# A planned order for the first and the last groups of a graph-attention layer, with Wq loaded by chunks and part of the weight work on GpSimd

## The reference, cut to what matters

```
h = maximum(layernorm(x), 0)
q, k, v = heads(h @ Wq + bq), heads(h @ Wk + bk), heads(h @ Wv + bv)
scores = q @ k.T / sqrt(64) + where(adj, 0, -9e15)
ctx = softmax(scores) @ v
out = x + ctx @ Wf + bf
```

## Time and profile before

| | |
|---|---|
| median of three runs | 478.66 us (477.88 to 484.44) |
| profiled execution: span from its first to its last instruction | 475.7 us |
| median less that span | 2.96 us |
| PE (TensorE matmul) busy | 460.9 us, 97% |
| DVE, ACT, POOL busy | 369.5, 364.8, 299.7 us |

### The profile page before, as it was taken

How to read it: one execution, slowest core, us unless ns; L and a number is a source line. 1 busy time by engine, 2 the same in 40 slices (tenths; PEclk the granted TensorE clock), 3 DMA queues, 4 the chain that set the end, 5 groups by cost and what they waited for, 6 DMA issues and landing times.

```text
span 475.7 us, 12878 instructions
## 1 busy us (share of the span) xinstructions
PE 460.9 (97%) x4454; PEld 275.6 (58%) x4454; DVE 369.5 (78%) x744; ACT 364.8 (77%) x813; POOL 299.7 (63%) x300
## 2 busy tenths in 40 slices
PE   4998999999999999999999999999999999999996
PEld 2854555556556564655657465565746556464763
DVE  4799997888679587786968778695786889677955
ACT  3677998789678877777888777887878968876950
POOL 3077576777676566686656678575767657634862
PEclk9799999999999999999999999999999999999999
DMA  8138599979969799795959969595978959966796
GB/s 294 66 83 162 97 167 170 161 154 194 210 108 199 167 160 230 132 221 116 221 119 198 199 122 227 112 222 92 191 176 129 263 109 162 217 107 148 137 197 169
DMA packets 219727, 78.56 MB, mean 165 GB/s; under 512 B 199584, under 2 KB 219680, under 8 KB 219680
## 3 DMA queue, kind: packets, MB, share of 16 engines
q1 hardware_dynamic: 209056, 65.43, 70.8%
q10 hardware_dynamic: 10624, 12.53, 9.9%
HBM read 16.19 MB, written 12.58 MB: 60 GB/s over the span
## 4 chain that ended last, share of the span: by engine, by line
PE 86%; DMA 4%; SPq 4%; DVE 2%; issue 1%; ACT 1%; POOL 1%; ACTq 0%; DVEq 0%
PE ps_proj L915 24%; PE ps_proj L917 24%; PE ps_proj L916 24%; PE ps_scores L997 6%; PE ps_ctx L915 2%; PE ps_ctx L916 2%; DMA pt_parts<-probs_parts 2%; PE ps_ctx L917 2%; SPq L474 2%; SPq L466 2%; DMA x_sb<-in_x 1%; DMA ht_parts<-h_pairs 1%; SPq L456 1%; DVE masked L751 0%; PE ps_ctx L1068 0%
## 5 line engine op out<-in xcount | busy, mean ns | idle before, releaser
L543 POOL TENSOR_TENSOR probs_parts<-probs,probs_parts 128x768 f16<-128x768 f32 x64 | 105.5, 1648 | 28.2 <-ACT probs_parts L645 28.1
L630 ACT ACTIVATE probs<-masked,neg_max 128x128 f32<-128x128 f32 x384 | 118.4, 389 | 2.3 <-DVE neg_max L760 2.1
L915 PE MATMUL ps_proj<-ht_parts,w_hi 128*128 128x512 f16 (+1 forms) x309 | 111.3, 364 | 3.3 <-DVE w_lo L833 2.0
L916 PE MATMUL ps_proj<-ht_parts,w_hi 128*128 128x512 f16 (+1 forms) x309 | 111.3, 364 | 0.0
L917 PE MATMUL ps_proj<-ht_parts,w_lo 128*128 128x512 f16 (+1 forms) x309 | 111.3, 364 | 0.0
L611 ACT ACTIVATE qkt_hi<-ps_proj,bias_qk 128x512 f16<-128x512 f32 x94 | 63.6, 682 | 37.9 <-PE ps_proj L917 37.2
L549 POOL TENSOR_TENSOR ctx_parts<-ctx_sb,ctx_parts 128x384 f16<-128x384 f32 x62 | 56.8, 917 | 53.3 <-ACT ctx_parts L651 53.0
L734 DVE SCALAR_TENSOR_TENSOR qkt_lo<-ps_proj,bias_qk,qkt_hi 128x512 f16<-128x512 f32 x94 | 69.0, 740 | 22.7 <-ACT qkt_hi L611 22.7
L528 POOL TENSOR_TENSOR h_pairs<-h_sb,h_pairs 128x384 f16<-128x384 f32 x60 | 55.8, 936 | 40.7 <-ACT h_sb L602 40.5
L751 DVE SCALAR_TENSOR_TENSOR masked<-ps_scores,score_unscale,mask 128x384 f32<-128x384 f32 x128 | 72.4, 609 | 8.8 <-PE ps_scores L997 8.8
L538 POOL TENSOR_TENSOR x_bf<-x_sb,b_out 128x384 f32<-128x384 f32 x64 | 63.4, 1002 | 9.8 <-DVE y_sb L783 9.5
(11 more groups left out here) (104 smaller groups left out, 916.4 us busy)
## 6 DMA issues: line engine op xcount, KB each, us to landing
y<-y_sb SPq DMA_DIRECT2D x64, 192.0 KB, 2.7
x_sb<-in_x ACTq DMA_DIRECT2D x56, 192.0 KB, 3.1
x_sb<-in_x SPq DMA_DIRECT2D x8, 192.0 KB, 7.8
pt_parts<-probs_parts SPq DMA_TRANSPOSE x64, 4.1
ct_parts<-ctx_parts SPq DMA_TRANSPOSE x62, 3.0
adj_sb<-in_adj ACTq DMA_DIRECT2D x14, 64.0 KB, 3.2
w_raw<-in_Wq ACTq DMA_DIRECT2D x1, 576.0 KB, 4.8
w_raw<-in_Wf SPq DMA_DIRECT2D x1, 576.0 KB, 7.6
```

What stands on the lines that cost most here:

```text
L543: nc.gpsimd.tensor_tensor(probs_parts[b][:, 1, :], probs[b % 2][:], probs_parts[b][:, 0, :], ALU.subtract).then_inc(probs_split, 1)
L630: last = nc.scalar.activation(probs[b % 2][:, u * N:(u + 1) * N], masked[b % 2][:, u, :], ACT.Exp, bias=neg_max[b % 2][:, u:u + 1])
L915: nc.tensor.matmul(to, a_hi, b_hi, start=first, stop=False)
L916: nc.tensor.matmul(to, a_hi, b_lo, start=False, stop=False)
```

## The change

What it does, in four parts.

1. **Beginning.** What stood ahead of the tables on DVE, ACT, PE and GpSimd becomes stages with turns, and all stages of groups 0 to 3 get new turns. Wq comes in three DMAs, a chunk each, and `reduce_first_rows` reduces each chunk apart. Wf is loaded after Wk, Wv and the x of group 1 instead of ahead of them. The sums over partitions use spare columns of the ctx bank. PE does 4 and 3 more warming matmuls (`keep_busy`) after the first sum. The four graphs of group 0 go one by one through the inverse deviation.
2. **GpSimd takes work.** The low parts of Wk and Wf are made there, by two instructions a chunk (`weight_scaled`: raw times scale; `weight_lo`: that less hi) instead of one on DVE. DVE keeps those of Wq and Wv (REST_BY_VECTOR).
3. **Value bias.** GpSimd multiplies Wf's chunks by the bias column (3 instructions) and adds them up (2); PE sums over the partitions by one float32 product with ones (`project_bias`) instead of three.
4. **Last groups.** All stages with turns above 100000 (the rest of groups 7 to 9, and groups 10 to 15) get new turns. The loop's body keeps its order on every engine.

```diff
-BANK_USES = [use[1:] for use in turns_of(("project_qk", "project_v", "project_out"))]
+BANK_USES = [("project_qk", 0, j) for j in range(C)] + [
+    use[1:] for use in turns_of(("project_qk", "project_v", "project_out"))]
+REST_BY_VECTOR = (0, 2)
+KEEP_BUSY = (15, 4, 3)
-            return (ps_proj[PROJ_BANKS - 1][:, 0:1], ps_scores[:, 0:1], ps_scores[:, 1:2], ps_ctx[0][:, 0:1])[n]
+            return ps_ctx[0][:, 512 - 4 + n:512 - 3 + n]
-        first_parts = (slice(0, 1), slice(1, 2), slice(2, B))
+        first_parts = tuple(slice(b, b + 1) for b in range(B))
...
-            for n, w in ((3, wf), (1, wk), (2, wv)):
-                sp.dma_start(w_raw[n][:], w.rearrange("(c p) n -> p c n", p=P)).then_inc(w_loaded[n], 16)
+            sp.dma_start(w_raw[1][:], wk.rearrange("(c p) n -> p c n", p=P)).then_inc(w_loaded[1], 16)
+            sp.dma_start(w_raw[2][:], wv.rearrange("(c p) n -> p c n", p=P)).then_inc(w_loaded[2], 16)
             for b in range(B):
                 sp.dma_start(x_sb[1][:, b, :], x_v[1, :, b, :]).then_inc(x_loaded[1][b], 16)
+            sp.dma_start(w_raw[3][:], wf.rearrange("(c p) n -> p c n", p=P)).then_inc(w_loaded[3], 16)
...
+            def bias_term(group, c, i):
+                if c == 0:
+                    pool.wait_ge(bias_loaded, 16)
+                    pool.wait_ge(w_loaded[3], 16)
+                nc.gpsimd.tensor_scalar(bias_terms[c][:], w_raw[3][:, c, :], bias_raw[:, 2, c:c + 1], None, ALU.mult)\
+                    .then_inc(bias_term_ready, 1)
+            def bias_sum(group, c, i):
+                pool.wait_ge(bias_term_ready, C + c)
+                nc.gpsimd.tensor_tensor(bias_terms[0][:], bias_terms[0][:], bias_terms[c + 1][:], ALU.add)\
+                    .then_inc(bias_term_ready, 1)
+            def weight_scaled(group, item, i):
+                n, c = divmod(item, C)
+                pool.wait_ge(scale_step, SCALE_STEPS * (n + 1))
+                if item >= C:
+                    pool.wait_ge(w_split[n - 1], c + 1)
+                nc.gpsimd.tensor_scalar(w_scaled[c][:], w_raw[n][:, c, :], w_scale[:, n:n + 1], None, ALU.mult)\
+                    .then_inc(w_scaled_ready[n], 1)
+            def weight_lo(group, item, i):
+                n, c = divmod(item, C)
+                pool.wait_ge(w_hi_ready[n], c + 1)
+                pool.wait_ge(w_scaled_ready[n], c + 1)
+                nc.gpsimd.tensor_tensor(w_lo[n][:, c, :], w_scaled[c][:], w_hi[n][:, c, :], ALU.subtract)\
+                    .then_inc(w_split[n], 1)
...
-            act.dma_start(w_raw[0][:], wq.rearrange("(c p) n -> p c n", p=P)).then_inc(w_loaded[0], 16)
+            wq_v = wq.rearrange("(c p) n -> p c n", p=P)
+            act.dma_start(w_raw[0][:, 0, :], wq_v[:, 0, :]).then_inc(wq_loaded[0], 16)
+            act.dma_start(w_raw[0][:, 1, :], wq_v[:, 1, :]).then_inc(wq_loaded[1], 16)
             act.dma_start(bias_raw[:], biases).then_inc(bias_loaded, 16)
+            act.dma_start(w_raw[0][:, 2, :], wq_v[:, 2, :]).then_inc(wq_loaded[2], 16)
...
-                for c in range(C):
-                    last = nc.tensor.matmul(ps_ctx[0][:, 0:H], bv_cols[:, c, :], w_raw[3][:, c, :],
-                                            start=c == 0, stop=c == C - 1)
-                last.then_inc(bv_projected, 1)
+                nc.tensor.matmul(ps_ctx[0][:, 0:H], plain_ones[:], bias_terms[0][:], start=True, stop=True)\
+                    .then_inc(bv_projected, 1)
```

One line of each table, as it changes (turns of group 0 on VectorE, and of group 15 on SP):

```diff
-        "statistics": (-122397, -68462, -68361, -37939), "aggregate": (-21870,), "inverse_deviation": (-81715,),
+        "statistics": (38400, 38470, 38530, 38540), "project_qk": (-69816, -69815, -69814, 39310, 39320, 39360),
-        "transpose_normed": (-383, -166), "project_qk": (-90, -89, 23455, 23456, 23827, 23828),
+        "normed_lo": (-49270, -49260, -49250, -49230), "transpose_normed": (-49380, -49370),
```

539 lines of the change are left out of this document (282 added, 257 removed).

## The result

The changed kernel took 487.38 us (median of four runs, 484.79 to 492.18) beside 479.50 us of the kernel before on the same chip (four runs, 477.88 to 484.44). The ratio is 1.0158, 95% interval 1.0111 to 1.0204; it is taken without the run of 492.18 us, whose mean granted clock was lower (0.986 beside 0.996). So the change made the kernel slower by about 1.6%, and whether by less than 2% the interval leaves open. The forecast was 473.9 us with a range up to 478.5; it had the wrong sign. The profiled execution, the shortest of the four, has a span of 483.1 us instead of 475.7. Another execution took 489.18 us, and no profile shows where; what follows is told of profiled executions.

A forecast was written before the change was run, and what follows sets the result against it. TensorE, busy 97% of the span, was taken to bound the kernel, its removable losses at the two ends. From 478.66 us: -2.0 - 1.35 - 0.8 + 0.5 - 1.1 = -4.75, so 473.9 us, range 470.5 to 478.5.

The forecast's parts named there:

- signs of being wrong: Clock of 0.50 anywhere after 11 us, GpSimd's new work at 0.9, or idle time appearing in groups 10 to 13.
- Term A: Beginning, to the start of Wk's product: near 20.1 instead of 22.10, -2.0 us; best -3.1, worst 0.
- Wq in chunks: Beginning: three reductions of 384 columns for one of 1152, two more issues on ACT; cost nothing.
- The named cover: Beginning: the wait for x was to hide the cost of Wq in chunks and the later Wf.
- Term B: Value bias in the beginning: TensorE's 6 instructions (2.0 us) become 2 (0.7), -1.35 us; 0 at worst.
- Term C: GpSimd's new work (+0.2) and the stall at 37 to 41 us (-1.0): -0.8 us; bounds -2.1 and +1.2.
- the rival that had GpSimd pace the beginning: Beginning: GpSimd's one-input work at two-input speed, and contention beside Wv's low parts; 476.2 us, chance 17%.
- Later in groups 1 to 3: Groups 1 to 3: VectorE was full before and lost TensorE nothing; it has 3.6 us less now.
- The stall at 37 to 41 us: TensorE's 2.11 us idle, partly for group 1's fourth transposed h; about 1.1 of it to stay.
- Term D: Middle, groups 10 to 13 in a new order on all engines: 0 to +1.5, taken as +0.5 us.
- The rival "slower": Last groups: the SP queue's new order holds up transposes and weigh_values; 480.6 us at 1.2 us a group, chance 11%.
- Term E: End: the last probabilities' transpose goes ahead of a store; -1.1 us, bounds -2.15 and +0.3.

The follow-up runs named there:

- e1: The changed kernel with the last groups' 712 turns (from 100000 on) as in the kernel before; 1.0135 of the kernel before.
- e2: The kernel before with the last groups' turns (from 100000 on) as in the changed kernel; 1.0066 of the kernel before.
- e10: New beginning, old last order, Wq by one transfer, Wk's low parts on VectorE; GpSimd's bias sums moved ahead of group 1's inverse deviation; 0.9992 of before.
- e3: e1 with group 1's shift on VectorE moved behind Wv's three low parts; 1.0091 of the kernel before.
- e13: e10 with the last groups' 712 turns in the changed kernel's order, as in e2; 1.0047 of the kernel before.
- e6: The kernel before with only the SyncE queue's 97 turns of the last groups in the changed order; 1.0183 of the kernel before.
- e7: The kernel before with the other engines' 615 turns of the last groups in the changed order, the SyncE queue's as before; 1.0643 of the kernel before.
- e8: The kernel before with the last graph's probabilities' transpose put ahead of one store on the SyncE queue; 1.0019 of the kernel before.

## Why the prediction was wrong

**The miss.** The forecast span was near 471 us and the profile has 483.1. Of these 12 us, 6.9 lie ahead of group 4 (terms A, B and C: 4.15 forecast as gain, 2.7 measured as loss) and 5.0 in the last groups (terms D and E: 0.6 forecast as gain, 4.4 measured as loss). Either alone would have put the time outside the range, as e1 and e2 show (484.6 and 481.3 us). All three of the signs of being wrong came: a clock of 0.50 after 11 us, GpSimd's new work over 0.9, idle time in groups 10 to 13.

**Term A (start of Wk's product, -2.0).** Mechanism and size right in the profiled execution: w_scale ready at 8.69 (8.6 said), clock 1.00 through the first products, Wk's product at 19.65 (20.1 said). That was partly luck. What I costed at nothing, Wq in chunks, was not nothing: in the four other profiles with chunks the third one came 1.2 to 2.6 us later, and w_scale started at 9.8 to 11.1 instead of 8.5. The named cover, the wait for x, doesn't cover it.

**Term B (bias, -1.35).** Right in size where nothing stands in its way: in e10 the two instructions take 0.81 us by their pipelined end, before the six took 2.18, 1.37 less. In the changed kernel TensorE reached them at half clock behind the waits for GpSimd, and in e3 it waited 1.76 us for them. I put the gain down and treated the bias's work on GpSimd as costing nothing beside; it stood, three terms of 1.24, ahead of group 1's inverse deviation.

**Term C (-0.8) is the step that failed**, in four places. (1) The price: a GpSimd tensor-scalar of 384 columns at 0.6 us, "one input, between the two"; it is 1.24, above my upper bound. A bound from a two-input operation wasn't a bound, and the rival that had GpSimd pace the beginning had the right mechanism with 2.3 us in place of some 7. I also misread what I quoted from the Trainium skill for this price (GPSIMD Engine Reference, sections 3 and 4.1): twice VectorE's own 0.61 is 1.2, and not the 0.92 that I put it at. The 1.24 agrees with that, and not with one-input operations at about line rate. (2) I had TensorE held up by 0.2 us behind group 1's shift; VectorE idled 4.99 at that shift. (3) Contention: I wrote that only the two sums stand beside low parts "and TensorE wants their result later than that". I looked at who wants the sums, not at what they do to VectorE: the low parts beside them took 1.4 us more and the shift 0.8, as e10 shows. Together TensorE waited 4.43 us where I had 0.2, and the clock's fall, which I looked for only in the first products, cost 1.4 us behind those waits. (4) "Later in groups 1 to 3 VectorE was full before and lost TensorE nothing": I put these groups at nothing although all their turns are new, and they cost 2.4 us of waits instead of 0.52; in e10, with the rest mended, still 2.2. No run takes the new turns of groups 1 to 3 apart. The stall at 37 to 41 us did go, wholly, but not by the plan: TensorE came late there. Where it comes early again, from e10 on, it waits 0.4 to 1.9 us for the same transpose, about the 1.1 said.

With the price avoided and the sums moved, the beginning gives what the plan promised in part: group 4 starts 1.5 to 2.8 us ahead of the mean of before's five profiles (which spread over 2.1) in the six kernels from e10 on that keep Wq whole and have the sums first; 4.15 was forecast.

**Term D (+0.5, at most +1.5)** was too small: +2.3 us of waits from 300 to 400 us in e13, where e10 has none. "I find no step whose consumer comes within 5 us of its producer" compared producers and consumers, and left out the queue between them, where a transpose waits behind stores for its turn and lands 4.8 to 7.2 us after it. The rival "slower" named just this; I gave it 11% because the old order had lost nothing with the same queue. That the old order lost nothing said that it was fitted, not that the queue had room: e6 and e7 show what a misfit costs.

**Term E (-1.1)** fell with e8: 0.84 us of that wait goes and 1.16 us come back one step later. The changed kernel has the same, 0.61 left of 1.39 and then 1.16. The bounds had no case in which the next transposes are late in its place. The term wasn't a sum either: its own items are -0.77 and +0.33, so -0.44, and the rest of the -1.1 has no row.

## What to carry to other kernels

An instruction that has no row in the trace can cost more than one that seems harder. Before a chain is built on it, take its worst case well above the nearest row, or write it in a form that has a row (the product with a broadcast column, 0.81 us for 1.24). Work given to GpSimd is not free for VectorE: put it where VectorE runs nothing with two SBUF inputs, check each such instruction, however small, and look at who is queued behind it. On a full DMA queue a wait that is moved away comes back at the next transfer in line unless the work ahead of it gets shorter; compare orders by the whole stretch, not by the wait.
